# Self-attention of a decoder layer: mask product ahead of the score product in the row maxima

## The reference, cut to what matters

```python
q, k = _rope(q, k)
scores = jnp.einsum('bqhd,bkhd->bhqk', q, k) * HEAD_DIM ** (-0.5)
causal = jnp.tril(jnp.ones((S, S), bool))
scores = jnp.where(causal[None, None], scores, jnp.finfo(scores.dtype).min)
attn = jax.nn.softmax(scores, axis=-1)
ctx = jnp.einsum('bhqk,bkhd->bqhd', attn, v).reshape(B, S, N_HEADS * HEAD_DIM)
x = x + ctx @ wo
```

## Time and profile before

| | us |
|---|---|
| median of 3 runs | 2498.14 |
| lowest and highest | 2497.02, 2505.15 |
| span of the profiled execution | 2499.1 |
| self attention in it | about 1333 to 1780 |

### The profile page before, as it was taken

How to read it: one execution, slowest core, us unless ns; L and a number is a source line. 1 busy time by engine, 2 the same in 40 slices (tenths; PEclk the granted TensorE clock), 3 DMA queues, 4 the chain that set the end, 5 groups by cost and what they waited for, 6 DMA issues and landing times. The chain is left out here.

```text
span 2499.1 us, 39149 instructions
## 1 busy us (share of the span) xinstructions
PE 2380.2 (95%) x15376; PEld 1538.7 (62%) x15376; DVE 1352.9 (54%) x2105; ACT 1351.0 (54%) x1714; POOL 925.5 (37%) x610
## 2 busy tenths in 40 slices
PE   8999999999999999999998899998899999999997
PEld 6877444444444444444334556555588899999885
DVE  6676534434443434443413655555565677776785
ACT  4332667667767777767994443433422366665221
POOL 1237655564465535564112333332033021221320
PEclk9999999999999999999999999999999999999999
DMA  6003775658465763766636000001154277775430
GB/s 219 17 18 108 221 193 117 173 154 209 99 173 147 197 169 83 189 168 166 172 87 219 1 1 18 1 18 54 59 169 154 86 241 245 240 238 184 145 118 34
DMA packets 206935, 331.46 MB, mean 133 GB/s; under 512 B 71264, under 2 KB 125792, under 8 KB 206560
## 3 DMA queue, kind: packets, MB, share of 16 engines
q1 hardware_dynamic: 188256, 252.80, 35.7%
q0 software_dynamic: 16336, 72.23, 8.9%
q10 hardware_dynamic: 2160, 3.93, 0.5%
HBM read 241.53 MB, written 99.42 MB: 136 GB/s over the span
## 5 line engine op out<-in xcount | busy, mean ns | idle before, releaser
L1052 ACT ACTIVATE A_c_prob<-c_psum 128x1024 f32<-128x1024 f32 x832 | 786.9, 1029 | 274.9 <-PE c_psum L1302 272.0
L982 POOL TENSOR_TENSOR E_c_roots<-E_c_roots,c_half 128x32 f32<-128x32 f32 (+1 forms) x70 | 363.2, 5190 | 401.0 <-DVE E_c_roots L1069 400.9
L1311 PE MATMUL c_psum<-A_c_prob,c_vq 128*17 128x512 f32 x3328 | 413.9, 597 | 8.6 <-DVE c_oT L1204 8.3
L137 PE MATMUL c_psum<-E_c_w,E_c_c 128*128 128x512 f32 x1248 | 312.4, 400 | 3.1 <-DVEq L1189 2.2
L1302 PE MATMUL c_psum<-c_qq,c_kq 64*128 64x512 f32 x1664 | 288.1, 437 | 17.9 <-ACT A_c_prob L1052 11.2
L137 PEld LDWEIGHTS c_psum<-E_c_w,E_c_c 128*128 128x128 f32 x1248 | 226.6, 188 | 124.3 <-issue 41.9
L1302 PEld LDWEIGHTS c_psum<-c_qq,c_kq 64*128 64x128 f32 x1664 | 136.5, 185 | 166.9 <-ACT A_c_prob L1052 92.8
L1108 DVE COPY E_c_unit<-c_psum 128x256 f32<-128x256 f32 x89 | 37.8, 425 | 328.8 <-PE c_psum L137 328.8
L2504 PE MATMUL m_psum<-A_m_dn_hi,A_m_a 128*128 128x512 f32 (+1 forms) x628 | 204.3, 394 | 2.2 <-DVE A_m_a L2301 2.2
L137 PE MATMUL m_psum<-R_m_t,m_up_hi 128*128 128x256 f32 (+1 forms) x1104 | 200.0, 283 | 0.0
L1311 PEld LDWEIGHTS c_psum<-A_c_prob,c_vq 128*17 128x17 f32 x3328 | 68.5, 96 | 187.6 <-issue 163.1
(11 more groups left out here) (316 smaller groups left out, 4221.4 us busy)
## 6 DMA issues: line engine op xcount, KB each, us to landing
c_kq<-kd SPq DMA_DIRECT2D x248, 208.0 KB, 6.1
kd<-S_c_t SPq DMA_DIRECT2D x96, 256.0 KB, 4.0
E_c_raw<-in_ctxT SPq DMA_DIRECT2D x89, 256.0 KB, 4.3
qd<-A_c_q SPq DMA_DIRECT2D x64, 256.0 KB
c_qq<-qd SPq DMA_DIRECT2D x64, 256.0 KB, 3.2
vd<-A_c_vt SPq DMA_DIRECT2D x104, 136.0 KB, 3.1
c_vq<-vd SPq DMA_DIRECT2D x31, 442.0 KB, 9.2
R_m_hs<-slots SPq DMA_DIRECT2D x23, 512.0 KB
```

What stands on the lines that cost most here:

```text
L137: mm = pe.matmul(out, a(c), b(c), start=first and i == 0, stop=last and i == len(terms) - 1)
L982: pool.tensor_tensor(rr[:, unit % RB, 0:n], ms[:, unit % RB, 0:n], half[:, 0:n], ALU.pow).then_inc(s_r, 1)
L1052: act.activation(prob[:, t % PB, 2 * (u % 2):2 * (u % 2) + 2, :], score_banks[u % 3], ACT.Exp, scale=XD ** -0.5).then_inc(s_ex, 1)
L1311: mm = pe.matmul(o_bank[32 * j:32 * j + VW, :], vq[:, q % 2, kt, j, :], prob[:, t % PB, j, :], start=kt == 0, stop=kt == CT - 1)
```

## The change

In `maxima` the two loops are exchanged. The four mask products are issued first and now carry `start=True`; the four score products follow, carry `start=False` and add to the banks, and the last of them raises the semaphore `s_max`. The waits ahead of the function, the shapes and the number of instructions stay. No other function is touched; what VectorE and ScalarE are given is the same as before, in the same order.

```diff
             def maxima(n, t):
                 p, L, ts = n % 2, (t + 1) * P, slice(t * P, (t + 1) * P)
                 for j in range(HPC):
-                    pe.matmul(s_bank[j][:, 0:L], qk_hi[rows[j], p, 0, ts], qk_hi[rows[j], p, 1, 0:L], start=True, stop=True)
+                    pe.matmul(s_bank[j][:, ts], ident16[:], neg[:], start=True, stop=False, skip_group_check=True)
                 for j in range(HPC):
-                    mm = pe.matmul(s_bank[j][:, ts], ident16[:], neg[:], start=False, stop=True, skip_group_check=True)
+                    mm = pe.matmul(s_bank[j][:, 0:L], qk_hi[rows[j], p, 0, ts], qk_hi[rows[j], p, 1, 0:L], start=False, stop=True, skip_group_check=True)
                 mm.then_inc(s_max, 1)
```

## The result

| | before | changed |
|---|---|---|
| median of 19 runs each | 2499.88 us | 2495.78 us |
| span of the profiled execution | 2499.1 us | 2494.1 us |
| first to last maximum (L1742) in it | 411.1 us | 403.4 us |

What follows compares the result with a forecast made beforehand. The prediction took TensorE to bound the stage, with the path running from the last projection product through the maximum; 45 calls x 0.11 us = 5.0 us gained, 2498.14 - 5.0 = 2493.1 us, range 2488.0 to 2500.0.

Steps and rivals of the forecast that it cites:

- What bounds the stage: Self attention: TensorE, busy 416.01 of 457.00 us; time removed between last projection product and the masks' end is gained in full.
- The gain is a passage from one use of the array to another: Behind a projection, in `maxima`: two passages up to the weighted products instead of three, with the same products.
- The passage is worth 0.11 us to the maximum: Behind a projection: the signal to VectorE comes 0.10 to 0.12 us earlier, taken as 0.11, in all four widths.
- 45 calls of 64: Calls of `maxima` that gain: 54 with PEld idle ahead of the first load, less those pinned by something else; 45 left.
- three kinds that were to gain nothing: Calls waiting for the exponential (9), rounds with values last (4), rounds with two output projections (3): each gains nothing.
- the prediction's rule: Which calls of `maxima` gain: those behind a projection not pinned by another wait, 0.11 us each, 45 of 64.
- Rows to columns costs nothing of its own: From score products to weighted products: this passage stays covered by the 0.42 us wait for the maximum, so counted at nothing.
- The first mask's weights load under the projection product: Behind a projection: first mask starts 0.22 us after the last projection product, without a passage; PEld's idle time there gone.
- Rival 1: First mask's weights load in the open behind the projection, about 0.10 us back in 45 rounds; 2498.1 us, chance 0.16.
- 5.0 us in all: Whole kernel: 45 calls x 0.11 us gained, profiled span from 2499.1 to 2494.1 us.
- Rival 3: Granted clock falls more often in the self attention; four further stretches at the lower level give 2506.7 us, chance 0.07.
- Its price of 3.4 us a fall: Loss per 10 us stretch at 0.66 of the full clock, from 1420 to 1430 us: 0.34 x 10 = 3.4 us.

Runs made afterwards that it cites:

- split masks: Against the changed kernel: masks of heads 0 and 1 ahead of the four score products, those of heads 2 and 3 behind; 2501.12 us, ratio to before 1.0012.
- masks on both sides: Against the changed kernel: the four mask products issued twice, once ahead of the score products and once behind; 2511.51 us, ratio to before 1.0054.
- both ahead: Against the changed kernel: the four mask products issued twice, both times ahead of the score products; 2507.34 us, ratio to before 1.0039.

## Why the prediction was right, point by point

- **What bounds the stage**: right. The counts of every wait stayed (55, 38, 9, 4), and what was taken out between the last projection product and the maximum came out of the stage, in more rounds than were counted (below).
- **The gain is a passage from one use of the array to another**: right, and shown by the split masks (passage back, gain gone) and by masks on both sides against both ahead (0.10 us for the passage alone).
- **The passage is worth 0.11 us to the maximum**: this term was mis-sized. It is 0.08 (1.14 to 1.06), in all four widths. Two things made it too large. The passage was taken as 0.10 to 0.12 from differences of two rows printed to 0.01 us, one of them against a spacing of 0.22; the projection products follow each other every 0.227 us in the trace's nanoseconds, the first score product 0.318 behind, so the passage is 0.09. And the maximum starts 0.05 us behind the modelled end of the score products, where it started 0.04 behind that of the masks: about 0.015 us is lost at the signal. What that is, the end's model or the score products themselves, stays open.
- **45 calls of 64**: the count is wrong, and that 45 x 0.08 is the 3.6 us between the undisturbed stages is partly luck. Two of the three kinds that were to gain nothing gained nothing. The third, the four rounds in which the values come last, gained 0.08 us each, because what the next step waits for there is the transposed maxima and not the weighted products. In the 40 intervals between the 17th and the 57th maximum the prediction's rule has 33 calls gain, 33 x 0.08 = 2.6 us; 36 intervals are shorter by 0.06 to 0.10 us (median of three profiles each), the other four by 0.03 at most, and the sum is 3.0. The fourth call of the stage was counted and gained nothing: in the first four calls a projection follows the products of `maxima`, so the passage that is saved ahead of the score products comes back behind them (from the projection product ahead to the one behind 1347.50 - 1346.71 = 0.79 us before, 1350.09 - 1349.27 = 0.82 changed), and the three intervals from the second to the fifth maximum are longer by 0.14 us together. That makes 48 calls that gain, some 3.7 to 4 us, less what the start loses.
- **Rows to columns costs nothing of its own**: right in that the wait covers it, though the passage itself isn't free. The weighted products start 0.37 us behind the first score product where the masks started 0.38 behind it: that passage is a passage like the others, and the wait behind it (0.44 us) covers it. The Trainium skill's "TensorEngine Tiling (Array Packing)", section Tiling Modes, says that a change of the tiling mode drains TensorE; the three kinds of passage that the rows here show, 0.09 to 0.10 us each, agree.
- **The first mask's weights load under the projection product**: half right. The trace writes that load at 1461.71, together with its product, not under the one before, and PEld's idle time fell only from 0.35 to 0.26 us; I had said it would be gone. But the mask starts 0.23 us after the projection product, 3 ns off the spacing of two projection products, so the load is in nobody's way. Rival 1 would have been at 0.3.
- **5.0 us in all**: right in the profile by luck. The profiled span moved by -3.6 (the change), -4.1 (two falls of the clock in before's stage and none in the changed one's: 411.1 against 407.0) and +2.8 (a later start of the stage), in all -4.9. The change's own part is 3.6 us, 0.14% of the time, and the 4.2 of the 19 runs has it inside its interval of 2.7 to 5.7.
- **Rival 3**, more falls of the clock: not shown, and not excluded. Its sign, a clock below 1.00 between 1430 and 1740 us, is absent from the first profile of the changed kernel and present in the two others, and absent from all three of before; the time did not go its way. Its price of 3.4 us a fall was too high for most: one cost 1.1 us, the two of before's first profile 4.1. As a source of spread it was underrated.

## What to carry to other kernels

Where TensorE goes from products on the whole array to products on a strip of rows or columns and back, count the passages and not only the products: put products that use the array alike next to each other, even if an accumulation then has to begin with the mask. It is worth about 0.09 us a passage, and only where the passage isn't already inside a wait, and where the engine that waits for the products isn't late for another reason; so count the calls by what they wait for first. Then follow the wait further: a product that is pinned by something else doesn't prove that the round gains nothing, if a later product waits for the signal that came earlier. And look at what stands behind the exchanged products, for there the passage can come back. A gain of a tenth of a percent is read from one place in several profiles and not from two spans: here the granted clock moved the span by more than the change did.

## What the runs showed of the hardware that was not expected

- A passage costs about the same whichever way it goes: 0.09 us from the whole array to rows of 32, 0.10 back (masks on both sides against both ahead). From rows of 32 to columns of 32 it costs no more.
- Four mask products that add to banks just written, or that open them, cost the same 0.22 us; so do score products that add to a bank in which a whole-array product has just written its block (0.45 us with 384 columns either way).
- In one and the same kernel the clock fell for a few microseconds in some executions and not in others, at about the same places, behind rounds in which TensorE had waited for the exponential (1.1 us in the rounds shown). Between the second and the third profile of before, both from one chip, one fell between 1420 and 1430 us and the other didn't. The stage took 407.0 to 411.1 us before and 403.4 to 409.0 changed.
